# The value steps of a group's order stand together in twos, scores and maxima units spread between them

## What is computed

```python
qkv = x @ w_qkv                                  # 512 -> 768
xq, xk = _apply_rope(xq), _apply_rope(xk)
keys, values = jnp.repeat(xk, 4, axis=1), jnp.repeat(xv, 4, axis=1)
scores = jnp.where(causal, einsum('bhsd,bhtd->bhst', xq, keys) * scale, -inf)
out = einsum('bhst,bhtd->bhsd', softmax(scores), values)
x = x + out @ w_o
x = x + scale * (layernorm(x) @ (kernel * 2 - 1))
```

## Time and profile before

| what | value |
|---|---|
| three runs | 1461.93, 1459.15, 1461.9 us, median 1461.9 |
| the profiled execution | 1458.99 us, its span 1457.0 us |
| mean granted TensorE clock | 0.978 of full |
| PE busy | 1322.6 us, 91% |
| DVE, ACT, POOL busy | 1040.6 us (71%), 942.2 us (65%), 383.0 us (26%) |
| chain that ended last | PE 67%, DVE 17%, ACT 6%, issue 6%, POOL 2% |
| costliest lines | exponentials (L909) 625.2 us on ACT; maxima (L1072) 694.1 us on DVE; value steps (L700) 325.8 us on PE |

### The profile page before, as it was taken

How to read it: one execution, slowest core, us unless ns; L and a number is a source line. 1 busy time by engine, 2 the same in 40 slices (tenths; PEclk the granted TensorE clock), 3 DMA queues, 4 the chain that set the end, 5 groups by cost and what they waited for, 6 DMA issues and landing times.

```text
span 1457.0 us, 28602 instructions
## 1 busy us (share of the span) xinstructions
PE 1322.6 (91%) x11076; PEld 773.6 (53%) x11076; DVE 1040.6 (71%) x1526; ACT 942.2 (65%) x1770; POOL 383.0 (26%) x591
## 2 busy tenths in 40 slices
PE   5988999999898899999999789999999889999998
PEld 4853444446775444444677444444478744444456
DVE  5677888845768788884566888888266587878737
ACT  4655777774665577777556567777646566777764
POOL 3431222210442122211144222222123422222212
PEclk9998999999999899999999999999999998999999
DMA  3000000001000000000220000000010000000002
GB/s 120 1 2 9 9 11 8 3 2 44 1 1 2 9 10 18 2 2 2 77 84 1 2 9 17 10 2 3 2 44 1 1 9 9 11 10 2 3 3 100
DMA packets 12981, 24.00 MB, mean 16 GB/s; under 512 B 1072, under 2 KB 4144, under 8 KB 12848
## 3 DMA queue, kind: packets, MB, share of 16 engines
q1 hardware_dynamic: 12848, 22.19, 4.6%
HBM read 16.94 MB, written 4.19 MB: 15 GB/s over the span
## 4 chain that ended last, share of the span: by engine, by line
PE 67%; DVE 17%; issue 6%; ACT 6%; POOL 2%; DMA 1%; DVEq 0%; SPq 0%; ACTq 0%; POOLq 0%
PE psO L700 20%; PE psE L679 13%; PE psM L564 12%; PE psM L637 12%; DVE mx L1072 9%; PE psM L547 3%; PE psE L617 3%; PE psO L617 2%; PE psM L644 2%; DVE stats L987 2%; ACT probs L909 2%; POOL attn L1217 1%; DVE attn L1098 1%; PE psM L664 1%; DVE qT L1037 1%
## 5 line engine op out<-in xcount | busy, mean ns | idle before, releaser
L909 ACT ACTIVATE probs<-psE 128x512 f32<-128x512 f32 x1152 | 625.2, 595 | 274.2 <-PE psE L679 267.1
L1072 DVE TENSOR_REDUCE mx<-psM 128x2 f32<-128x768 f32 (+4 forms) x704 | 694.1, 1025 | 126.9 <-PE psM L644 96.0
L637 PE MATMUL psM<-kT,qT 62*128 62x384 f32 (+5 forms) x1536 | 305.3, 411 | 52.2 <-DVE mx L1072 35.4
L700 PE MATMUL psO<-probs,v_grp 128*32 128x512 f32 (+3 forms) x3072 | 325.8, 513 | 2.3 <-POOL probs L1270 2.2
L1270 POOL TENSOR_SCALAR_AFFINE_SELECT probs<-probs 128x512 f32<-128x512 f32 x256 | 159.3, 634 | 584.1 <-ACT probs L909 543.9
L679 PE MATMUL psE<-qT,kT 64*128 64x512 f32 (+3 forms) x1536 | 287.9, 412 | 24.2 <-ACT probs L909 19.6
L637 PEld LDWEIGHTS psM<-kT,qT 62*128 62x128 f32 x1536 | 148.3, 189 | 174.5 <-DVE mx L1072 132.0
L679 PEld LDWEIGHTS psE<-qT,kT 64*128 64x128 f32 x1536 | 131.7, 188 | 173.9 <-ACT probs L909 131.5
L644 PE MATMUL psM<-mask_b 64*128 64x64 bf16 x2048 | 120.9, 198 | 0.0
L700 PEld LDWEIGHTS psO<-probs,v_grp 128*32 128x32 f32 x3072 | 68.1, 109 | 88.0 <-issue 62.7
L564 PE MATMUL psM<-wq_hi,xT_hi 128*128 128x512 f32 (+1 forms) x384 | 98.8, 379 | 16.0 <-ACT vs L873 9.5
(11 more groups left out here) (81 smaller groups left out, 1246.3 us busy)
## 6 DMA issues: line engine op xcount, KB each, us to landing
probs<-in_w_qkv SPq DMA_DIRECT2D x5, 1536.0 KB, 6.7
xs<-in_x SPq DMA_DIRECT2D x8, 512.0 KB, 4.1
xn<-in_w_o SPq DMA_DIRECT2D x16, 256.0 KB, 2.6
out_x<-xs SPq DMA_DIRECT2D x8, 512.0 KB, 2.9
qT<-nm_rows SPq DMA_DIRECT2D x128, 8.0 KB
probs<-in_w_ffn SPq DMA_DIRECT2D x1, 256.0 KB, 7.3
attn<-in_mask SPq DMA_DIRECT2D x1, 160.0 KB, 9.1
sin_s<-in_sin SPq DMA_DIRECT2D x1, 128.0 KB, 6.8
```

Of the source, the lines that this page charges most:

```text
L637: return pe.matmul(psM[:, 2 * pair + h % 2, to:to + k1 - k0], qT[lo:lo + MAXROW, g, qt // QT_PER_CHUNK, h // 2, qt % QT_PER_CHUNK * P:(qt ...
L700: ins = pe.matmul(psO[VW * j:VW * (j + 1), off:off + w], v_grp[:, kb, :], probs[:, (g * NS + s) % PSLOTS, at(j), to:to + w], start=s in (0 ...
L909: act.activation(probs[:, (g * NS + s) % PSLOTS, at(heads[0]):at(heads[0]) + len(heads), 0:w], psE[:, n % SRING, 0:w * len(heads)].rearran ...
L1072: dve.tensor_reduce(to, src, AX.X, ALU.max, negate=True).then_inc(ring_used.sem, 1)
```

## The change

Only the text of `GROUP_ORDER` is edited. The words are the same; their order is not. PV.8 and PV.9, PV.0 and PV.1, PV.3 and PV.4, PV.5 and PV.6 stand next to each other; PV.2 and PV.7 stand alone. N.0.1 stands before S.13 in place of after S.14, N.1.0 after S.2 in place of before it, O.1.-1 between S.8 and S.9 in place of after S.6, O.0.0 between S.15 and S.16 in place of after S.7, and OC.1.-1 before S.2 in place of after it.

```diff
 GROUP_ORDER = """
-S.0 U.0 U.1 PV.8.-1 S.1 U.2 PV.9.-1 N.1.0 S.2 OC.1.-1 U.3 U.4 U.5
-S.3 U.6 S.4 PV.0.0 U.7
-S.5 U.8 PV.1.0 U.9 S.6 O.1.-1 OC.0.0 PV.2.0 S.7 U.10 O.0.0
-S.8 U.11 U.12 S.9 PV.3.0 U.13
-S.10 U.14 PV.4.0 S.11 U.15 U.16 S.12 U.17
-S.13 PV.5.0 S.14 N.0.1 U.18 S.15 U.19 PV.6.0
-S.16 U.20 U.21 S.17 PV.7.0 X
+S.0 U.0 U.1 S.1 PV.8.-1 PV.9.-1 OC.1.-1 S.2 N.1.0 U.2 S.3 U.3 S.4 U.4 U.5 PV.0.0 PV.1.0 U.6 S.5 U.7
+S.6 U.8 PV.2.0 OC.0.0 U.9 S.7 U.10 U.11 S.8 O.1.-1 S.9 U.12 U.13 S.10 U.14 S.11 U.15 PV.3.0 PV.4.0
+S.12 U.16 N.0.1 S.13 U.17 U.18 S.14 PV.5.0 PV.6.0 U.19 S.15 O.0.0 S.16 U.20 U.21 X S.17 PV.7.0
 """
```

## The result

| | median | runs | mean granted clock of the runs |
|---|---|---|---|
| before | 1457.2 us | 20 (1450.3 to 1463.8) | 0.978 to 0.980 (median by chip, where it is listed) |
| after | 1466.7 us | 20 (1462.3 to 1471.0) | 0.981 |

The ratio is 1.0068, its 95% interval 1.0055 to 1.0081: the change makes the kernel 9.5 us slower (8 to 12). With twenty runs the median of before is 1457.2 and not the 1461.9 of the three runs that the prediction had, so the difference is larger than the two levels 1461.9 and 1466.7 suggest.

The account below looks back on a forecast made before the run. PE, 91% busy, was bound by its work, score spacing after exponentials and the ring of maxima awaiting DVE. Per group, 0.5 us less work plus 0.75 standing gave +0.28; 24 groups, 6.7 us: 1468 us, range 1452 to 1481.

Parts of the forecast that it names:

- junction: Where two value steps become neighbours on PE: each saves 0.13 to 0.14 us, four save 0.55 us a group.
- The sum: Over 24 edited groups: 0.5 us less work, 0.75 new standing, +0.28 us each, 6.7 us in all.
- The prediction's sign: In the profile after: distances between DVE's X steps of 28.1 to 28.3 us where the clock is full.
- the cover of the copy of w_o: ACT's copy behind S.8, 0.6 us in four groups, partly hidden in waits: 0 to 0.3 us a group, taken as 0.
- the work of units ahead of another kind of step: PE's maxima units in the hand-laid order: priced at 0.24 to 0.41 us each.
- hand count: New order laid out from S.0 to the next S.0: 18 score distances summing to 28.07 us, 3.7 of it standing.
- the number of falls: Granted clock fell in 9 of 24 groups, one seen 1.55 us longer; count taken as unchanged.
- (a): Junctions win: PE standing stays 3.0 us a group, 12 us gain, 1450 us; decides at 3.5 us standing; chance 0.11.
- (b): The two cancel: standing 3.4 to 3.6 us, group within 0.12 us of now, 1459 to 1465 us; chance 0.20.
- (c): Clock falls change: in every group 1491 us, none 1454; chance 0.13 for more, 0.09 for far fewer.
- the knot at U.5, U.6 and S.4: Old order's PE standing before the clock fall: 0.8, 0.4 and 0.2 us, 1.4 us reckoned.
- (d): Cover of PV.1, 0.1 to 0.3 us for POOL's masks, breaks: 1472 to 1475 us; within the forecast's 0.47.

Follow-up runs that it names:

- join34: Kernel before with only PV.3 moved behind U.14, directly ahead of PV.4: 1468.5 us against 1457.9, ratio 1.0083.
- join89: Kernel before with only PV.8 moved behind U.2, directly ahead of PV.9: 1454.0 us against 1457.9, ratio 0.9977.
- the pair of half kernels: Old and changed orders, both with ACT's exponentials and DVE's reductions about halved and denominators not inverted: 1370.0 us old, 1360.4 us changed.
- after_wo10: Changed kernel with ACT's copy of w_o behind S.10's exponentials in place of S.8's: 1460.7 us against 1457.9 of before, ratio 1.0017.
- after_half: Changed order with exponentials and reductions about halved and denominators not inverted: 1360.4 us, against 1370.0 for the old order halved alike.
- undo34: Changed kernel with PV.3 put back between S.9 and S.10, away from PV.4: 1460.2 us against 1455.0 of before, ratio 1.0038.
- oc_behind: Changed kernel with copy OC.1.-1 put back behind the exponentials of S.2: 1469.4 us against 1455.7 of before, ratio 1.0092.
- both spread ones: Before reordered, value steps alone, at most one between scores: 1414.3 us, ratio 0.9712; same with w_o's copy behind S.10: 1414.0 us, 0.9726.
- loose_knot: Kernel before with S.3 ahead of U.5, U.6 behind PV.0 and U.7 behind S.5, no pair: 1453.1 us against 1455.7, ratio 0.9980.

## Why the prediction was right, point by point

**Direction and place.** Right: slower, by scores that come too close together and by new waits of units for DVE at U.11 (0.43 us) and U.17 (0.26). In sum PE waits less for DVE than before and more for ACT. The pair saves 0.14 us a junction as priced from the earlier trace rows; join34 shows a tight pair costing 0.5 to 0.6, join89 one with room costing nothing, and the pair of half kernels shows that the order gains where ACT and DVE have half the work.

**Distances.** Forecast and measured, S.0 to S.1 and so on, in the group of S.4 at 193.37 us (the first four from the group behind it):

| S.n to S.n+1 | 0 | 1 | 2 | 3 | 4 | 5 | 6 | 7 | 8 |
|---|---|---|---|---|---|---|---|---|---|
| forecast | 1.28 | 1.83 | 1.28 | 1.18 | 3.25 | 1.18 | 1.47 | 1.42 | 1.18 |
| measured | 1.26 | 1.86 | 1.27 | 1.19 | 3.28 | 1.15 | 1.48 | 1.43 | 1.18 |

| S.n to S.n+1 | 9 | 10 | 11 | 12 | 13 | 14 | 15 | 16 | 17 |
|---|---|---|---|---|---|---|---|---|---|
| forecast | 1.20 | 1.18 | 2.52 | 1.25 | 1.29 | 2.63 | 1.18 | 1.32 | 1.43 |
| measured | 1.49 | 1.20 | 2.61 | 1.19 | 1.52 | 2.69 | 1.24 | 1.27 | 1.40 |

The sums are 28.07 and 28.71. Fifteen of the eighteen are within 0.06. The group shown is the longest of the 20 (28.72 from X to X). In the group from 245.56 to 273.90 us, which has no copy of w_o, the measured sum is 28.34, with 1.26 at S.9, 2.62 at S.11 and 1.45 at S.13.

**The terms that were mis-sized.** The sum said +0.28 us a group and 6.7 in all; at full clock it is +0.65 in the groups with a copy of w_o and +0.42 in the others, 13.9 us over 16 and 8 groups. The prediction's sign was 28.1 to 28.3 us; the groups without the copy just miss it (28.31 to 28.35) and those with it miss it by 0.25 and more. Two steps of it failed in size. First, the cover of the copy of w_o: I took 0 out of "0 to 0.3", and it is near the upper end, 0.24 (S.9 to S.10, 1.49 for 1.20; 1.26 in after_wo10). Second, the work of units ahead of another kind of step was priced from steps ahead of a unit or score: U.15 ahead of PV.3 takes 0.43 us (204.91 to 205.34) and not 0.33, and S.13 to S.14 has 0.16 to 0.23 more, part wait at U.17 and part work. The two are 0.26 or more; the forecast had added 0.13 to its hand count of 28.07, and the rest is the other 0.14.

**The clock.** I took the number of falls as unchanged, for want of a row. In groups 2 to 6 they went: no long group among 20 where before has five. Over the runs the difference is smaller, a clock of 0.981 against 0.978 to 0.980. In the 25 runs of before on one chip the time goes from 1446.2 us at a mean clock of 0.987 to 1461.0 at 0.975, 12 us for 0.01; 0.001 to 0.003 are 1 to 4 us. So of the 13.9 us 10 to 13 should be left, and measured are 9.5 (8 to 12): the sum closes within its error, and at its lower end. The two misses lay on opposite sides, and the forecast of 6.7 came as near as it did in part by that. The 1468 came within 1.3 us of the measured 1466.7 by luck of another kind as well: its base, 1461.9, was 4.7 us above the median of twenty runs. The prediction also priced every group with a fallen clock at 1.55 us more. That fits the five groups behind it, but group 1 takes 4.2 to 4.4 us more than 27.9 in three rounds of before, and 5.2 more than 28.57 in two of after, with several falls in each.

**The rivals.** (a), PE work decides, is refuted by after itself and by join89. That saved changes of the array's shape save 0.14 us each holds, but it does not decide the time. In after_half, where ACT and DVE are late for less, 0.24 of the 0.5 us come through. Its deciding point, 3.5 us of standing a group, was passed: 28.33 less the 24.3 of work that the prediction counted is 4.0. (b), the two cancel, is what join89 does. (c): a stretch of 6 us without a value step does not lower the clock by itself, since the changed kernel has that in each group and no fall in groups 2 to 6. What stands ahead of the falls in these groups is the knot at U.5, U.6 and S.4. The three profiled kernels that keep it at full work, before, join34 and join89, have 5, 4 and 4 falls there. Read in steps of 1 us, all thirteen start 6.4 to 7.4 us behind X, which is at or right behind the end of the knot (in before, X is at 192.57, U.5 starts behind its wait at 197.78 and S.4 at 199.36). The seven without it that do the full work (after, undo34, after_wo10, oc_behind, both spread ones and loose_knot) have none in 140 groups. Falls elsewhere are not explained by it: group 1 has them in every one of these ten traces, others come in the last group and outside the groups, and their causes were not tried. (d) did not come, by little: in the group shown the second block of mask 1 ends near 195.2 us and PV.1 follows PV.0 near 195.4. The weight loads of value steps wait 17.0 us in all for POOL (30 times, before 3.8 and 8 times), beside the running step ahead of them; PE itself stood for POOL there 2.2 us in all, before and after.

## What to carry to other kernels

A saving on the busiest engine is worth what is left once the engines that it feeds keep their pace. Here scores follow each other at 1.14 to 1.20 us at the closest, and units wait for the reduction two before, so a kind of work that keeps PE alone for 1 us belongs between scores, one at a time, and not in twos; the even spread of one long step to one short won 2.9% where pairing lost 0.7%. Lay the new order out by its distances (work, shortest distance, ring) before saving junctions, price each step by what follows it, and count secondary copies on the late engine at their full length.

## What the runs showed of the hardware that was not expected

The granted clock did not go with the amount of PE's standing alone. The order with the knot loosened has longer groups at full clock than before (28.07 against 27.91 us) and yet, over its runs, more clock (0.986 against 0.980) and slightly less time. In groups 2 to 6 the clock fell only behind one bunch of waits, some 1.4 us of standing in 2.5 us, in 13 of the 60 groups that have it at full work, and in none of 140 without. The evenly spread order got some 15 of its 44 us from the clock. The spread of repeated runs of one kernel, 1446 to 1461 us for before, goes with the granted clock too. Kernels that differ by under 1% are compared better by their lengths of a group at full clock than by single executions, and where the clock falls cannot be told from one profiled execution: even group 0, which no edit touched, took 27.71 to 31.29 us in these ten traces.
